# Weight pieces of two experts prepared in the routing stage, on ScalarE and GpSimd; 66 pieces in place of 77 in the first attention

## The reference, cut to what matters

```
x = x + L0_xattn(norm(x), ctx, Wq, bq, Wk, bk)        # q and k from ctx, x_m = x . softmax(q k^T)^T
x = x + L0_ffn(norm(x), gate_w, gate_proj, up_proj, down_proj)
x = x + L1_xattn(norm(x), ctx, positions, ...)        # 32 heads, rotary positions
x = x + L1_ffn(norm(x), Wg, Wu, Wd, Wr, LoRA of 8 experts)

def L0_ffn(x):                                         # 8 experts, 2 for each token, 352 hidden
    top_w, sel = top_k(x @ gate_w.T, 2); top_w = softmax(top_w)
    h = silu(x @ gate_proj[e].T) * (x @ up_proj[e].T)  # for every expert e
    return sum over the two chosen e of top_w * (h @ down_proj[e].T)
```

## Time and profile before

| | |
|---|---|
| median of 3 runs | 1787.26 us (1785.75 to 1790.98) |
| the profiled execution's own time | 1789.83 us |
| its span | 1788.1 us |
| mean granted TensorE clock | 0.946 |
| busy in the span | TensorE 1621.3 us (91%), weight loads 1189.5 (67%), VectorE 1066.6 (60%), ScalarE 785.5 (44%), GpSimd 459.1 (26%) |
| first attention, 77 jobs | 0 to 159 us |
| router loop | 159 to 188 us |
| routing stretch, 11 jobs | 188 to 227 us |
| expert tiles | 227 to 494 us |
| second attention and second feed-forward layer | 494 to 1788 us |

### The profile page before, as it was taken

The page is one execution under the profiler, slowest core; times in us unless marked ns, Lnnn a source line. Parts: engine busy times, 40 slices in busy tenths (PEclk is TensorE's granted clock), DMA queues, the critical chain, the costliest instruction groups (busy, mean ns, idle before and its releaser), DMA issues. The chain is left out here.

```text
span 1788.1 us, 25118 instructions
## 1 busy us (share of the span) xinstructions
PE 1621.3 (91%) x8534; PEld 1189.5 (67%) x8534; DVE 1066.6 (60%) x1957; ACT 785.5 (44%) x1239; POOL 459.1 (26%) x424
## 2 busy tenths in 40 slices
PE   5987599999949869999999989779999999999995
PEld 4776589999837633334333356548888888888884
DVE  5886622222259858988889835635555547454454
ACT  4653232333245417887878843433333333232331
POOL 1210022223247740111110011222232223233331
PEclk9998699999979968999999999989999999999997
DMA  8995126472147662222222111433233345422211
GB/s 288 323 365 200 40 96 247 175 276 82 61 171 270 190 182 52 64 68 73 73 73 69 42 19 71 164 114 126 79 127 127 88 169 227 146 89 79 75 45 59
DMA packets 109516, 236.14 MB, mean 132 GB/s; under 512 B 39808, under 2 KB 53248, under 8 KB 100688
## 3 DMA queue, kind: packets, MB, share of 16 engines
q1 hardware_dynamic: 103152, 214.06, 35.9%
q0 software_dynamic: 6240, 20.45, 3.4%
HBM read 274.71 MB, written 93.32 MB: 206 GB/s over the span
## 5 line engine op out<-in xcount | busy, mean ns | idle before, releaser
L1977 DVE TENSOR_REDUCE r_top<-r_ring 128x1 f32<-128x512 f32 x512 | 324.1, 681 | 35.9 <-PE r_ring L1874 31.7
L1960 ACT ACTIVATE r_probs<-r_st 128x1024 f32<-128x1024 f32 x256 | 248.0, 1021 | 49.9 <-PE r_st L1861 47.3
L2921 DVE TENSOR_TENSOR attn<-attn,f_u 128x512 f32<-128x512 f32 x132 | 90.8, 688 | 192.8 <-PE f_u L48 132.3
L48 PE MATMUL m_bank<-w_place,m_xT 128*128 x936 | 166.0, 326 | 4.2 <-DVE m_xT L1189 3.2
L2846 ACT ACTIVATE attn<-f_g 128x512 f32<-128x512 f32 x132 | 78.9, 598 | 180.2 <-PE f_g L56 124.3
L48 PEld LDWEIGHTS m_bank<-w_place,m_xT 128*128 128x128 f32 x936 | 151.3, 189 | 8.3 <-issue 5.0
L2874 POOL TENSOR_TENSOR wout_split<-attn,wout_split 128x512 fp32r<-128x512 f32 x66 | 85.6, 1297 | 200.7 <-ACT wout_split L2850 200.7
L1895 PE MATMUL r_out<-r_probs,early_v 128*17 128x512 f32 x1024 | 136.4, 605 | 0.5 <-ACT r_probs L1960 0.3
L48 PE MATMUL f_g<-late_xnT,late_weights 128*128 128x512 f32 x528 | 129.5, 395 | 7.2 <-PEq L2104 7.2
L2874 POOL TENSOR_TENSOR f_hidS<-attn,f_hidS 128x512 fp32r<-128x512 f32 x66 | 85.5, 1296 | 194.9 <-ACT f_hidS L2850 194.9
L48 PE MATMUL f_u<-late_xnT,late_weights 128*128 128x512 f32 x528 | 129.4, 394 | 0.0
(11 more groups left out here) (330 smaller groups left out, 3073.1 us busy)
## 6 DMA issues: line engine op xcount, KB each, us to landing
w_place<-expert_split SPq DMA_DIRECT2D x72, 1408.0 KB
w_place<-expert_split SPq DMA_DIRECT2D x36, 1024.0 KB
late_w_dram<-late_weights SPq DMA_DIRECT2D x11, 1920.0 KB, 8.0
expert_split<-w_place SPq DMA_DIRECT2D x10, 1408.0 KB, 9.0
w_place<-expert_split SPq DMA_DIRECT2D x36, 384.0 KB
late_weights<-late_w_dram SPq DMA_DIRECT2D x11, 1024.0 KB
late_weights<-late_w_dram SPq DMA_DIRECT2D x11, 896.0 KB
early_slots<-y_rows SPq DMA_DIRECT2D x16, 512.0 KB
```

What stands on the lines that cost most here:

```text
L48: last = nc.tensor.matmul(out, l, r, start=(i == 0), stop=(i == len(passes) - 1))
L1960: nc.scalar.activation(probs[k][:, 2 * pair:2 * pair + 2, :], st_ps[pair][:], ACT.Exp, scale=SCALE).then_inc(exp_done, 1)
L1977: nc.vector.reduce_max(top[g % 2][:, q, h:h + 1], ring(place(q, h))[:], AXIS_X).then_inc(max_read, 1)
L2921: nc.vector.tensor_tensor(hid[:, c, var, :], hid[:, c, var, :], u_ps[c][:], ALU.mult).then_inc(hid_done, 1)
```

## The change

- The first attention prepares 6 jobs first and 15 in each batch (2, 2, 2 and 0, 3, 3, 3): 66 in place of 77.
- The other 22, those of the last two experts, are done in the routing stretch. TensorE turns two ahead of the transposes of the last logits, six behind them, the other fourteen between the rank matmuls and the map matmuls. The ring has five banks of PSUM in place of three.
- VectorE has no part in these 22. ScalarE copies the bank twice, once as the high part and once in full into one of the six buffers of `rows` in SBUF (`hi_and_copy`). GpSimd subtracts the high part from that copy (`lo_from_copy`).
- ScalarE does all 22 ahead of the exponential of the routing weights. It waits for the stores of `xn_rows` from the buffer that it overwrites, and from the seventh job on for GpSimd's subtraction six jobs before.
- GpSimd gathers the first rows only when its 22 subtractions are done.
- SyncE issues the loads of the last three units behind the 16 stores of `xn_rows`.
- TensorE waits for all copies before it turns the first gathered tile (bank 0 is in the ring), and for all subtractions only before the second tile.

```diff
+    def hi_and_copy(self, job, bank, copy):
+        _, _, (n_rows, n_cols), (hi, lo) = self.parts(job)
+        self.nc.scalar.activation(hi, bank[0:n_rows, 0:n_cols], ACT.Copy)
+        return self.nc.scalar.activation(copy[0:n_rows, 0:n_cols], bank[0:n_rows, 0:n_cols], ACT.Copy)
+
+    def lo_from_copy(self, job, copy):
+        _, _, (n_rows, n_cols), (hi, lo) = self.parts(job)
+        self.nc.gpsimd.tensor_tensor(lo, copy[0:n_rows, 0:n_cols], fp32(hi), ALU.subtract).then_inc(self.split, 1)
-PREP_FIRST, PREP_A, PREP_MIX = 5, (2, 2, 3), (0, 3, 4, 4)
+PREP_FIRST, PREP_A, PREP_MIX = 6, (2, 2, 2), (0, 3, 3, 3)
...
-        x_banks, prep_banks = bank[0:2], [bank[i] for i in (2, 3, 6)]
+        x_banks, prep_banks = bank[0:2], [bank[i] for i in (0, 1, 2, 3, 6)]
...
             pool.wait_ge(x_turned, TILES + 1)
+            for job in range(FIRST, JOBS):
+                pool.wait_ge(copied, job - FIRST + 1)
+                weights.lo_from_copy(job, w_copy(job))
             pool.wait_ge(routed, 1)
+            pool.wait_ge(weights.split, JOBS)
...
-            for unit in range(3 * (E0 - 1), weights.UNITS):
-                weights.load(sp, unit)
             for i in range(TILES):
                 sp.wait_ge(n.xn_ready, i + 1)
                 sp.dma_start(xn_rows[i * P:(i + 1) * P, :], rows[:, i % XN, :]).then_inc(xn_out[i % XN], DMA)
+            for unit in range(3 * (E0 - 1), weights.UNITS):
+                weights.load(sp, unit)
...
+            def turn_weights(start, stop):
+                for job in range(start, stop):
+                    wait_count(pe, copied, job - FIRST + 1 - len(prep_banks))
+                    weights.turn_into(pe, job, w_bank(job))
             router(TILES - 1)
-            for job in range(FIRST, FIRST + 3):
-                weights.turn(pe, job, prep_banks)
+            turn_weights(FIRST, FIRST + 2)
             turn_logits(TILES // TPB - 1)
+            turn_weights(FIRST + 2, EARLY)
...
             last.then_inc(rank_ready, 1)
-            for job in range(FIRST + 3, FIRST + 6):
-                weights.turn(pe, job, prep_banks)
+            turn_weights(EARLY, JOBS)
...
-            for job in range(FIRST + 6, JOBS):
-                weights.turn(pe, job, prep_banks)
...
             pe.wait_ge(routed, 2)
+            pe.wait_ge(copied, JOBS - FIRST)
             turn_x(0)
-            pe.wait_ge(weights.split, JOBS)
...
-            for job in range(FIRST, FIRST + 6):
-                weights.hi(act, job, prep_banks)
+            act.wait_ge(weights.split_out[weights.place_of(E0 - 2)], weights.stores_before(E0 - 2))
+            for job in range(FIRST, JOBS):
+                act.wait_ge(weights.turned, job + 1)
+                if job - FIRST < XN:
+                    i = job - FIRST
+                    act.wait_ge(xn_out[i], DMA * len(range(i, TILES, XN)))
+                else:
+                    act.wait_ge(weights.split, job + 1 - XN)
+                weights.hi_and_copy(job, w_bank(job), w_copy(job)).then_inc(copied, 1)
             act.wait_ge(gap_ready, 1)
             nc.scalar.activation(t.e[:], t.gap[:], ACT.Exp).then_inc(gap_exp, 1)
-            for job in range(FIRST + 6, JOBS):
-                weights.hi(act, job, prep_banks)
```

More of the change, by code:

```diff
@@ L1080, in _ @@
             nc.vector.tensor_copy(ltri[:], ltri_f[:]).then_inc(ltri_ready, 1)
-            for job in range(FIRST, FIRST + 3):
-                weights.lo(dve, job, prep_banks)
             dve.wait_ge(logits_ready, TILES // TPB)
```

14 lines of the change are left out of this document (12 added, 2 removed).

## The result

The changed kernel takes 1800.13 us in the median of 8 executions (1796.46 to 1802.99), the kernel before 1789.01 in 8 beside it (1783.53 to 1797.84). The ratio is 1.0057, with an interval of 1.0036 to 1.0079: slower by some 11 us. The profiled execution took 1800.67 us (span 1798.2).

What follows compares the result with a forecast made beforehand. The routing stretch was taken as bound by one chain of small dependent VectorE operations, the first attention by no single engine. -8.5 + 8.1 + 2.0 = +1.6 us on the median of 1787.26 gave 1789 us, range 1779 to 1796.

Steps and rivals of the forecast that it cites:

- The first attention: Twelve pieces leave the four batches and one joins the opening group: -8.5 us, between -3.4 and -10.
- the wait of 3.25 us: First attention at 104.97: TensorE's wait for a piece being loaded would go, with VectorE's 2.71 us taken as gained.
- The routing stretch, the gain: All VectorE's pieces leave the routing stretch: -3.8 us by plain durations.
- The routing stretch, the cost: VectorE's two-SBUF-input operations alternate with GpSimd's subtractions: eighth one-hot group 8.3 us late, first expert matmul +8.1.
- Step 1: Copied logits to one-hots: eight two-input VectorE operations beside eight GpSimd pieces take 7.6 us, one-hots 2.1 late.
- Step 2: Rank matmuls end at 201.45; VectorE resumes near 201.6, 0.6 us earlier than before.
- Step 4: After the ranks: GpSimd's fourteen pieces take 14.6 us, VectorE's turns add 6.6; last one-hot group at 225.3, 8.3 late.
- The clock: First expert matmuls after TensorE's idle of some 6 us run at 1.2 instead of 2.4 GHz: +2.0 us.
- GpSimd hides: Rival, routing stretch: VectorE isn't held, stretch gives -3.8, clock costs 2.0; -10.3 in all, 1777 us; chance 0.12.
- Little from the first attention: Rival: removed pieces mostly covered other waits and the load is late elsewhere; only -3.4 there, 1794 us; chance 0.2.
- the held operations of the top two: Sign, routing stretch: 128-wide two-input operations take 0.6 to 0.9 us and not 0.29, ending with GpSimd's.
- the 1280-wide operations and the one-hot groups: Sign, routing stretch: 1280-wide operations take 2 us or more, one-hot groups come 1.4 us apart.

Runs made afterwards that it cites:

- run 2: The changed kernel with 77 pieces in the first attention as before, only the last expert's 11 by ScalarE and GpSimd: 1794.83 us, ratio 1.0015.
- run 12: The changed kernel with each of an expert's three matrices stored as soon as it is split: 1792.38 us, ratio 1.0021.
- 13: The kernel before with each matrix stored as soon as it is split: 1786.54 us, ratio 0.9986.
- run 11: The changed kernel with the first of the eight subtractions ahead of the ranks on 96 partitions only: 1802.25 us, ratio 1.0088.
- run 10: The changed kernel with GpSimd's subtraction of each third down-matrix piece on 128 partitions in place of 96: 1795.55 us, ratio 1.0036.
- run 14: The changed kernel with each matrix stored when split and the router's logits, scores, places, tile numbers and token-number copy in PSUM: 1776.96 us, ratio 0.9924.
- run 1: The changed kernel without GpSimd's 22 subtractions, transposes and ScalarE's copies kept: 1782.43 us, ratio 0.9957.
- 9: The changed kernel with eleven pieces instead of eight turned ahead of the rank matmuls: 1791.68 us, ratio 1.0015.
- run 7: The changed kernel with three copy buffers in place of six: 1800.81 us, ratio 1.0058.
- Run 15: The kernel of run 14 plus 28 useless transposes on TensorE between the map matmuls and the gathered rows: 1774.53 us, ratio 0.9938.
- 3: The changed kernel with two small arrays, slot_tile and slot_low, in PSUM in place of SBUF: 1795.84 us, ratio 1.0038.
- 8: The changed kernel with one more 128x128 product of two SBUF tensors on VectorE ahead of L1149: 1798.82 us, ratio 1.0048.

## Why the prediction was wrong

**The first attention** was put at -8.5. The edit did put it that far ahead for a while: 8.2 us at the start of the last batch's tokens. The step that failed is the load: I had the wait of 3.25 us go and took 2.71 as gained, and a longer one (5.10) stood 27 us later. In the eleven profiles with this attention code, except those with the new stores, the first transposed token tile behind it comes 2.4 to 5.2 us earlier than in the kernel before, 3.7 in the mean; and in the one with the old attention code (run 2) 1.7 earlier, which shows what a single profile is worth. The prediction had this as a rival ("the load is late at another place", -3.4), and the cause it missed is that one store of 4.3 MB stands in front of a load on the same queue. Runs 12 and 13 show it: with the stores cut in three the gain is 7.2 us (-9.9 against -2.7).

**The routing stretch, the gain.** -3.8 by plain durations: logits to eighth group is 22.7 us without subtractions against 26.2, so -3.5. Right.

**The routing stretch, the cost,** was put at +8.3 at the eighth group with these gains in it, and was +12.0 (from -5.2 to +6.8). Point by point:
- Step 1, the top two: 7.6 us from the logits to the one-hots, measured 8.0 (184.42 to 192.41). The 352-wide subtraction at 0.87 is right too (0.89, run 11).
- Step 2, ranks: 4.05 us from the one-hots to VectorE's next operation, measured 3.94.
- Step 4, from there to the eighth group: 23.7 us, measured 27.4. Here is the failure. "Each wait for one and hold the next" holds for every operation but one. With no 96-partition subtraction (run 10) the same stretch takes 23.9 us, as worked out.

That 23.9 meets 23.7 so closely is partly luck. In run 10 GpSimd's fourteen take 19.4 us and VectorE ends 2.4 behind them; the prediction had 21.2 and 0.6. It also left out the three `tensor_scalar`, which are held there for 1.6 us in all.

The 3.5 us between 27.4 and 23.9 are a shut-out of 10 us less the alternation that it replaces: while L1149 waits, GpSimd runs at full pace and is done early, and all that follows is free. In the traces taking the shut-out away shortens the stretch by 3.6 us and two buffers by 2.7, while only PSUM (run 14) or no subtraction (run 1) takes back the other 12 to 13 as well: the alternation itself was the larger cost, and the prediction had it.

What sets off the shut-out is shown by three runs: it is gone where the 96-partition operation stands last in its run (9), gone where no operation is on 96 partitions (10), and it appears in the other run where one is put there (11). Other numbers of partitions were not tried. Why it does is not shown. The Trainium skill ("GPSIMD Engine Reference", Specifications) gives each of eight cores 16 partitions of its own. By that, two cores have no work in a 96-partition operation and could begin the next while six still run, so that from then on GpSimd's operations overlap and there is no moment with all cores idle, until the next 96-partition operation lets the six catch up. This would fit the turn that VectorE got just ahead of the fourteenth, which is on 96 partitions. With three buffers (run 7) one request got in and the next did not. Its trace would fit too: as the fourth subtraction ended (204.59), ScalarE was still writing the copy for the sixth (until 204.62), so that cores one subtraction ahead would have had nothing to do just then. No run here looks inside GpSimd, so this stays an idea that the rows don't contradict.

**The clock** was put at +2.0. The first expert tile ran at 0.50 as predicted, its loads took 2.26 us more. The shift is +5.6 at the first expert matmul (232.43 against 226.85) and +7.8 at the first product of the hidden layer: the slow tile costs 2.3 us. At the eighth group it is +6.8, so 1.2 us came back ahead of the first tile, which the prediction didn't have; the gather alone comes 2.4 us behind the eighth group, where it was 3.4. Run 15 prices the clock at 3.0 in the profile; its medians say 2.4, its ratios nothing.

**The rest.** The terms sum to +6.7 at the last expert tile in the profile, against +1.6. Behind it the code is the same, and up to VectorE's last operation the shift still changes by -2.0 to +8.2 us among the profiles, by +5.0 in this one. Windows of one such stretch, the kernel before and then the changed one:

```profile
1050.00:1215.00 165.00, 134.61 (x623) 99.11 (x622) 86.47 (x212) 59.92 (x108) 37.04 (x36) 0.90 0.27 97
```

```profile
1050.00:1215.00 165.00, 131.37 (x594) 95.89 (x587) 83.48 (x216) 57.70 (x104) 32.88 (x34) 0.87 0.28 98
```

0.90 against 0.87 of 165 us is 5 us of clock. The run with all on 128 partitions has 0.90 here and drifts by 3.6 all the same. So between +6.7, which has causes, and the measured +11, whose interval begins at 6.4, some us stay without one: I can't say whether they belong to the change.

Of the rivals, "GpSimd hides" was wrong by the whole mechanism. "Little from the first attention" was right in its mechanism and gave 1794; the shut-out, which no rival had, came on top.

Of the signs that the prediction named, the held operations of the top two and the low clock came. The router's first matmul behind the barrier came 5.1 us earlier and not 8 (155.86 against 160.93), a wait of 5.10 for a raw piece was left, and the 1280-wide operations and the one-hot groups were not held, since the shut-out had let GpSimd finish ahead of them. In run 10 they are held as forecast (2.11 and 1.4 us).

## What to carry over

Where VectorE and GpSimd both read SBUF, look for each VectorE operation whether an input or the output can lie in PSUM: that took back nearly all of the 16.7 us lost here (run 14), more than any order or buffering. Where further GpSimd operations follow at once, run its elementwise operations on all 128 partitions rather than 96, and look in the profile for a tiny VectorE operation that takes microseconds. And when a load wait vanishes from its place, ask which big store stands in front of the next load on the same queue.

## What the runs showed of the hardware

- A VectorE operation with two SBUF inputs, or a `tensor_scalar` from SBUF to SBUF, waits for the GpSimd subtraction in progress (0.50 to 1.36 us in place of 0.18 to 0.29). For the `tensor_scalar` no row of the kernel before showed it. The two then alternate, every 0.935 us for 352 columns (0.89 with nobody in between). With one side in PSUM and at most one SBUF input it isn't held: 0.20 for 32 columns, 0.30 for 128, 1.49 for 1280.
- One GpSimd operation on 96 partitions with further ones ready behind it: one VectorE operation was shut out for 6.91, 8.57, 8.74, 10.07 and 10.89 us (runs 11, 7, 3, the changed kernel, 8). With two copy buffers it wasn't (1.42), and with 128 partitions throughout it was 1.36 at most for operations of up to 128 columns.
- A long VectorE row need not be a slow operation: L1149 took 10.07 us, its work is 0.18 (run 1).
- A load behind a store of 4.3 MB on the same queue: TensorE waited 5.10 us for it. With the store in three parts no wait for a weight load was left (run 12).
- TensorE's clock: after an idle of 5.95 us the first expert tile ran at 0.50 (run 14), with TensorE kept busy there at 1.00 (run 15); the 24 weight loads took 6.28 and 3.82 us.
